# A graph and expert network on one core: expert results added to the output rows by accumulating transfers

## What is computed

```python
h = xf @ shared_w1 + shared_b1
z = swiglu5(h, ...) @ shared_w2 + shared_b2
w, idx = jax.lax.top_k(softmax(xf @ gate_w + gate_b), 2)     # w normalised to sum 1
cw = sum(one_hot(idx, 16) * w)
te = swiglu5(xf @ expert_w1[e] + expert_b1[e], ...)          # for every e
oe = te @ expert_w2[e] + expert_b2[e]
out = x + z + sum_e cw[:, e] * oe[e]
```

## Time and profile before

| what | value |
|---|---|
| median of 3 runs | 988.98 us (986.0 to 990.35) |
| the profiled execution, own time | 987.39 us |
| its span, first to last instruction | 985.6 us |
| PE busy (matmuls) | 853.1 us, 87% |
| DVE busy | 509.0 us, 52% |
| ACT busy | 234.1 us, 24% |
| POOL busy | 78.6 us, 8% |
| mean granted TensorE clock | 0.943 |
| HBM read, written | 101.97 MB, 16.92 MB |

### The profile page before, as it was taken

One profiled execution on the slowest core, in us unless ns is written; L12 is line 12 of the kernel. 1 busy time (PEld: TensorE's weight loads), 2 busy tenths in 40 slices (PEclk: granted clock), 3 DMA queues, 4 the chain that ended last, 5 costly groups with the idle time before them and its releaser, 6 DMA issues.

```text
span 985.6 us, 12333 instructions
## 1 busy us (share of the span) xinstructions
PE 853.1 (87%) x3638; PEld 572.8 (58%) x3639; DVE 509.0 (52%) x934; ACT 234.1 (24%) x483; POOL 78.6 (8%) x127
## 2 busy tenths in 40 slices
PE   4887699999999949679998688999998989999890
PEld 2444478888888826368887543544554545555440
DVE  7988681431431797890246958434343343433362
ACT  2555321431431024242112121102121211212110
POOL 2000000000000300000000010111011110110180
PEclk9999779999999978889999598999999999999996
DMA  4720000000000010001001120427754593314163
GB/s 141 223 101 1 1 1 1 0 1 1 1 1 1 27 45 1 1 1 43 1 3 60 66 91 0 168 99 276 279 176 154 190 352 92 148 53 154 39 178 118
DMA packets 38647, 80.98 MB, mean 82 GB/s; under 512 B 7304, under 2 KB 7554, under 8 KB 38602
## 3 DMA queue, kind: packets, MB, share of 16 engines
q1 hardware_dynamic: 27850, 60.55, 17.9%
q0 software_dynamic: 6720, 12.49, 4.3%
q10 hardware_dynamic: 4032, 7.34, 2.0%
HBM read 101.97 MB, written 16.92 MB: 121 GB/s over the span
## 4 chain that ended last, share of the span: by engine, by line
PE 70%; DVE 11%; DMA 5%; ACT 5%; issue 4%; POOL 2%; ACTq 1%; SPq 0%; DVEq 0%; POOLq 0%
PE PS L893 18%; PE PS L1108 13%; PE PS L923 8%; PE PS L1141 7%; PE PS L827 5%; PE PS L1016 5%; DMA WB<-in_b 3%; PE PS L962 3%; PE PS L1096 3%; PE PS L1126 2%; ACT CTR L607 1%; ACT YF L754 1%; POOL GA L576 1%; POOL GB L576 1%; DMA GB<-y_dram,slot_i 1%
## 5 line engine op out<-in xcount | busy, mean ns | idle before, releaser
L893 PE MATMUL PS<-CTR,YH 125*128 125x500 f32 (+1 forms) x480 | 167.0, 363 | 3.8 <-DVE YL L1405 3.4
L893 PE MATMUL PS<-CTR,YL 125*128 125x500 f32 (+1 forms) x480 | 165.1, 359 | 0.0
L1108 PE MATMUL PS<-WB,YF 128*128 x448 | 150.4, 489 | 7.5 <-DMA WB<-in_b 5.0
L1108 PEld LDWEIGHTS PS<-WB,YF 128*128 128x128 f32 x448 | 84.0, 190 | 76.7 <-issue 24.7
L893 PEld LDWEIGHTS PS<-CTR,YH 125*128 125x128 f32 x480 | 92.1, 192 | 22.5 <-DVE YL L1405 9.8
L893 PEld LDWEIGHTS PS<-CTR,YL 125*128 125x128 f32 x480 | 92.6, 193 | 12.6
L1141 PE MATMUL PS<-WB,YF 128*128 x168 | 79.4, 609 | 12.5 <-ACT YF L754 11.2
L827 PE MATMUL PS<-ET 125*128 125x130 f16 x494 | 71.0, 291 | 15.7 <-ACT CTR L607 8.2
L1438 DVE TENSOR_TENSOR ZL<-PS,ZH 128x500 fp32r<-128x500 f32 (+1 forms) x36 | 21.1, 591 | 93.1 <-ACT ZH L657 93.1
L754 ACT COPY YF<-PS 128x384 f32<-128x384 f32 (+1 forms) x38 | 18.1, 477 | 213.8 <-PE PS L1118 213.8
L827 PEld LDWEIGHTS PS<-ET 125*128 125x128 f16 x494 | 40.4, 116 | 47.0 <-ACT CTR L607 26.5
(11 more groups left out here) (324 smaller groups left out, 1214.8 us busy)
## 6 DMA issues: line engine op xcount, KB each, us to landing
WB<-in_w SPq DMA_DIRECT2D x28, 1536.0 KB
WB<-in_w SPq DMA_DIRECT2D x28, 768.0 KB
WB<-in_b SPq DMA_DIRECT2D x28, 384.0 KB
y_dram<-YF ACTq DMA_DIRECT2D x28, 256.0 KB
y_dram<-XTF SPq DMA_DIRECT2D x1, 4352.0 KB, 14.5
X<-in_x SPq DMA_DIRECT2D x1, 2500.0 KB
xn_dram<-XN SPq DMA_DIRECT2D x1, 2500.0 KB
out<-X SPq DMA_DIRECT2D x10, 250.0 KB
```

What stands on the lines that cost most here:

```text
L893: mm = nc.tensor.matmul(dest, lhs, rhs, start=(t == 0 and h == 0), stop=(t == NT - 1 and h == 1))
L1108: mm = nc.tensor.matmul(PS[:, 2 * k + h, 0:INTER], xgt[:, k, f, :], WB[:, bass.ds(off + (f * H2 + h * INTER), INTER)], start=(f == 0), sto ...
```

## The change

All ten shared blocks now come before the experts (`EARLY = NT`, 10). SP stores the ten tiles of `X` to `out` between the loads of the third and the fourth block's weights. The expert results no longer go to `y_dram`: POOL issues for each block one indirect transfer that adds the 128 rows of `yo` to their rows in `out` in memory. `out` gets 128 extra rows, one for each partition; an unused slot adds its zeros there. The extra rows are set to zero at the start and cut off on the host. Each such transfer waits for the one before (`scattered`), and each is issued behind the gather for the third next block (`AHEAD = 3`). ACT's `result` now waits for the transfer of two blocks before in place of the store. `GA`, `GB`, their gathers and sums, and `store` are gone. DVE works out the destination table `home` before it signals `tables_ready`.

```diff
-EARLY = 6
+EARLY = NT
+AHEAD = 3
...
-            sp.dma_start(y_dram[SURE * BS:NB * BS, :].rearrange("(b p) d -> p b d", p=BS),
-                         XT[:, 0:D].rearrange("p (o d) -> p o d", o=1).to_broadcast([128, NB - SURE, D])
-                         ).then_inc(zeroed, 16)
+            sp.dma_start(out[N:N + BS, :], XT[:, 0:D]).then_inc(zeroed, 16)
...
-            for b in range(4):
+            for b in range(NWB):
+                load_weights(b // 2, b % 2, b)
+            for t in range(NT):
+                sp.wait_ge(z_added, t + 1)
+                sp.dma_start(out[t * NP:(t + 1) * NP, :], X[0:NP, t, :]).then_inc(out_stored, 16)
+            for b in range(NWB, 4):
                 load_weights(b // 2, b % 2, b)
...
-            for t in range(NT):
-                sp.wait_ge(sum_ready, t + 1)
-                sp.dma_start(out[t * NP:(t + 1) * NP, :], X[0:NP, t, :]).then_inc(out_stored, 16)
+            sp.wait_ge(zeroed, 16)
             sp.wait_ge(out_stored, 16 * NT)
...
-            for b in range(2):
-                gather(0, b, b)
+            def scatter(k, b):
+                if isinstance(b, int):
+                    turn, seen = b + 1, 16 * b
+                else:
+                    turn, seen = pool.to_reg(b + 1), pool.to_reg(b * 16)
+                if not (isinstance(b, int) and b < 1):
+                    pool.wait_ge(scattered, seen)
+                pool.tensor_copy(dest_i[:, k:k + 1], home[:, bass.ds(b, 1)]).then_inc(dest_ready, 1)
+                pool.wait_ge(out_stored, 16 * NT)
+                pool.wait_ge(yo_ready, turn)
+                pool.wait_ge(dest_ready, turn)
+                pool.indirect_dma_start(out[:, :], bass.IndirectOffsetOnAxis(dest_i[:, k:k + 1], 0), yo[:, k, :], None,
+                                        compute_op=ALU.add).then_inc(scattered, 16)
+
+            for b in range(AHEAD):
+                gather(0, b % 2, b)
+            pool.wait_ge(zeroed, 16)
             last = last_pair(pool)
-            with pool.Fori(1, NB // 2) as i:
+            gather(0, 1, AHEAD)
+            scatter(0, 0)
+            with pool.Fori(2, NB // 2) as i:
                 with pool.If(i < last + 1):
-                    for k in range(2):
-                        gather(i, k, i * 2 + k)
-
-            all_stored = pool.to_reg(last * 16 + 16)
-            pool.wait_ge(tables_ready, 1)
-            pool.wait_ge(stored[0], all_stored)
-            pool.wait_ge(stored[1], all_stored)
-            for t in range(NT):
-                for k, dest in enumerate((GA, GB)):
-                    pool.indirect_dma_start(dest[0:NP, t, :], None, y_dram[:, :],
-                                            bass.IndirectOffsetOnAxis(slot_i[0:NP, k, t:t + 1], 0)
-                                            ).then_inc(back_in[t // 2], 16)
...
+                    gather(i, 0, i * 2)
+                    scatter(1, i * 2 - AHEAD)
+                    gather(i, 1, i * 2 + 1)
+                    scatter(0, i * 2 + 1 - AHEAD)
+            ending = pool.value_load(eb_i[0:1, 3, 1:2], min_val=SURE - AHEAD, max_val=NB - AHEAD)
+            for j in range(AHEAD):
+                scatter((j + 1) % 2, ending + j)
+            pool.wait_ge(scattered, pool.to_reg(last * 32 + 32))
...
                 act.wait_ge(y_done, b + (EARLY + 1))
                 if not first:
-                    act.wait_ge(stored[k], i * 16)
+                    act.wait_ge(scattered, act.to_reg(b * 16 - 16))
...
-            shared_up(0, last * 2 + (EARLY + 2), EARLY)
             turn_act(1, last * 2 + (EARLY + 1))
             down(last, 1, last * 2 + 1)
-            for j in range(NT - EARLY):
...
-            v.tensor_copy(wslot[:, :], PS[:, 4, NB:2 * NB]).then_inc(tables_ready, 1)
+            link(v.tensor_copy(wslot[:, :], PS[:, 4, NB:2 * NB]))
+            link(v.tensor_scalar(padrow, nodef[:, 0:1], float(N), None, ALU.add))
+            link(v.tensor_scalar(filled, wslot[:, :], 0.0, None, ALU.not_equal))
+            link(v.scalar_tensor_tensor(out=filled, in0=PS[:, 4, 0:NB], scalar=padrow, in1=filled,
+                                        op0=ALU.subtract, op1=ALU.mult))
+            v.tensor_scalar(home, filled, padrow, None, ALU.add).then_inc(tables_ready, 1)
...
-            def gathered_sum(t):
...
-            def last_sum(t):
...
-    out = nc.dram_tensor("out", (N, D), F32, kind="ExternalOutput").ap()
+    out = nc.dram_tensor("out", (N + BS, D), F32, kind="ExternalOutput").ap()
...
-    return r.results[0]["out"]
+    return r.results[0]["out"][0:N]
```

More of the change, by code:

```diff
@@ L160, in build @@
         assert R_ZL + NWB * WBUF * 4 <= R_SW and 2 * ROWB <= NWB * WBUF * 4
-        GA, GB = [at(n, r, [128, NT, D]) for n, r in (("GA", R_ZL), ("GB", R_ZL + ROWB))]
         used = [0]
@@ L265, in build @@
         tt_ps, tt_ready, y_done, yo_ready = sem("tt_ps"), sem("tt_ready"), sem("y_done"), sem("yo_ready")
-        stored = [sem("stored0"), sem("stored1")]
+        dest_ready, scattered = sem("dest_ready"), sem("scattered")
         zeroed = sem("zeroed")
@@ L269, in build @@
         cw_ps, cwt_ready = sem("cw_ps"), sem("cwt_ready")
-        back_in = [sem(f"back_in{g}") for g in range(NT // 2)]
-        sum_ready, out_stored = sem("sum_ready"), sem("out_stored")
+        out_stored = sem("out_stored")
         xn_dram = nc.dram_tensor("xn_dram", [N, D], F32, kind="Internal")
-        y_dram = nc.dram_tensor("y_dram", [NB * BS, D], F32, kind="Internal")
         w1f = FFNR[0:FK3, 0:W1C]
@@ L349, in build @@
         idx = sb("idx", [128, 2], I32)
+        dest_i = sb("dest_i", [128, 2], I32)
+        padrow, filled = rcarve(1), rcarve(NB)
+        home = rcarve(NB).bitcast(I32)
         idx_ready = sem("idx_ready")
@@ L572, in _ @@
-            pool.wait_ge(stored[0], all_stored)
-            pool.wait_ge(stored[1], all_stored)
-            for t in range(NT):
-                for k, dest in enumerate((GA, GB)):
-                    pool.indirect_dma_start(dest[0:NP, t, :], None, y_dram[:, :],
-                                            bass.IndirectOffsetOnAxis(slot_i[0:NP, k, t:t + 1], 0)
-                                            ).then_inc(back_in[t // 2], 16)
-            for g in range(NT // 2):
-                pool.wait_ge(back_in[g], 16 * 4)
+                    gather(i, 0, i * 2)
@@ L767, in sigmoid @@
                 nc.scalar.activation(ss[k][0:rows], hb[k][0:rows, 0:H2:2], ACT.Sigmoid, scale=alpha).then_inc(gate_sig, 1)
-            def store(i, k, b):
-                act.wait_ge(yo_ready, b + 1)
-                act.dma_start(y_dram[bass.ds(b * BS, BS), :], yo[:, k, :]).then_inc(stored[k], 16)
             def result(i, k, b, first=False):
@@ L793, in _ @@
                 with act.If(i < last + 1):
-                    store(i, 0, i * 2 - 2)
                     turn_t(1, i * 2 + (EARLY - 1))
@@ L801, in _ @@
                         result(i - 1, 1, i * 2 - 1)
-                    store(i, 1, i * 2 - 1)
                     turn_t(0, i * 2 + EARLY)
@@ L805, in _ @@
                     result(i, 0, i * 2)
-            store(0, 0, last * 2)
             turn_t(1, last * 2 + (EARLY + 1))
-            sigmoid(0, last * 2 + (EARLY + 2))
             result(last, 1, last * 2 + 1)
-            store(0, 1, last * 2 + 1)
-            for j in range(NT - EARLY):
-                turn_t(j % 2, last * 2 + (EARLY + 2 + j), NP)
-                if j + 1 < NT - EARLY:
-                    sigmoid((j + 1) % 2, last * 2 + (EARLY + j + 3))
         @block.tensor
@@ L1168, in _ @@
                 shared_up(p % 2, p, p)
-                if p == EARLY - 3:
+                if p == 3:
                     pe.wait_ge(slots_ready, 1)
@@ L1790, in _ @@
             link(v.tensor_scalar(ebf[0:1, 3, 0:1], ebf[0:1, 3, 0:1], -MAGIC, None, ALU.add))
-            link(v.tensor_copy(eb_i[0:1, 3, 0:1], ebf[0:1, 3, 0:1]))
+            v.tensor_copy(eb_i[0:1, 3, 0:1], ebf[0:1, 3, 0:1])
+            link(v.tensor_scalar(eb_i[0:1, 3, 1:2], ebf[0:1, 3, 0:1], 2.0, float(2 - AHEAD), ALU.mult, ALU.add))
             z_add(0, 0)
@@ L1797, in _ @@
             v.tensor_copy(tok[:, :], PS[:, 4, 0:NB])
-            v.tensor_copy(wslot[:, :], PS[:, 4, NB:2 * NB]).then_inc(tables_ready, 1)
+            link(v.tensor_copy(wslot[:, :], PS[:, 4, NB:2 * NB]))
[4 more added lines that the diff above has]
+            v.tensor_scalar(home, filled, padrow, None, ALU.add).then_inc(tables_ready, 1)
             dve.wait_ge(tables_ready, 1)
             last = last_pair(dve)
[L1801 to L1806, removed]
+            for p in range(4, EARLY):
+                z_add(p - 2, p - 2)
+                units(p % 2, p)
             rows_copy(0, 0)
@@ L1821, in _ @@
                     units(1, i * 2 + (EARLY + 1), i * 2 + 1, next_rows)
-            def gathered_sum(t):
-                dve.wait_ge(back_in[t // 2], 16 * 4)
-                link(v.tensor_tensor(GA[0:NP, t, :], GA[0:NP, t, :], GB[0:NP, t, :], ALU.add))
-            def last_sum(t):
```

## The result

The changed kernel takes **978.73 us**, the median of 6 runs (973.36 to 983.83), against 989.71 for six runs of the kernel before. The ratio is 0.9903, with a 95% interval of 0.9881 to 0.9925: faster by 0.75 to 1.2%. The forecast was 977. The profiled execution took 980.72 us; its span is 979.0, where 973.7 was forecast, at a mean granted clock of 0.943, as before. In medians the gain is 11.0 us, in the spans of the two profiled executions 6.6: that of the change lies 2.0 us above its median of 978.73, that of the kernel before 2.3 under its median of 989.71.

A forecast was written before the change was run, and what follows sets the result against it. TensorE was 70% of the chain, then a 58.6 us tail of gathers, sums and stores. Block 26's end, 916.82 + 40.8 + 2.8 = 960.4, plus two scatters gave span 973.7, 11.9 less; on the median's level 977, range 969 to 999.

The forecast's parts named there:

- Shared blocks, +40.8: Four shared blocks moved ahead of the experts delay the expert stage by 4 x 10.19 = 40.8 us, the change's price.
- What leaves the tail: 20 gathers, 11.27 us of landing, 20 additions and 10 stores leave the end; stores of X are covered before the next load.
- the 4.2: Last expert block: turn, copy and matmuls take 4.2 us after its activation chain, as for block 26.
- DVE's row table: Five small operations on DVE, about 1 us with waits, beside DVE's 1.99 us wait for TensorE: nothing paid.
- The fill: The fill of y_dram at the start shrinks to 128 rows; its waiter, ACT, comes long after: no effect.
- ACT's stores: ACT loses 28 stores, issued after results for which nobody on the chain waits: no effect.
- L = 5: Each adding scatter on POOL takes 5 us from issue to landing, range 3.2 to 11.3; the chain waits for data.
- the list of what would show it: Signs for the later profile: scatter landings of 4 to 8 us; wrong if POOL idles on its own scatter mid-stage.
- Traffic, 2.8 us: The adding pass lengthens four TensorE waits on weight loads by 0.7 us each, 2.8 us; range 0 to 8.4.
- The sum's last term: At the end, from the last scatter's landing at 973.3 to the span's end: 0.4 us for last wait and wakes.
- the slow one: Rival: POOL's chain of 28 scatters bounds the expert stage from a mean step of 9.54 us; slower, chance 0.22.
- Its variant on two engines: Scatters run on two DMA engines, L = 12, about 1080 us; chance 0.04 of the slow rival's 0.22.

The follow-up runs named there:

- x3: Kernel before with only the order changed: all ten shared blocks ahead of the experts, results still through y_dram, gathers and sums at the end; 1021.82 us, ratio 1.0343.
- x4: Changed kernel with the large fill of y_dram put back at its old place, nothing reading it; 980.54 us, ratio 0.9922 to the kernel before.
- x2: Changed kernel with the scatters as plain writes, without the addition; 973.93 us, ratio 0.9865 to the kernel before.
- x1: Changed kernel with the last wait for the scatters on ACT, with one tiny copy behind it, not on POOL; 973.08 us, ratio 0.9859 to the kernel before.
- x5: Changed kernel with four weight buffers, the fourth in the place of the dead shared weights; 967.10 us, ratio 0.9783 to the kernel before.
- x7: Changed kernel with AHEAD = 2, each scatter issued one gather earlier; 1125.68 us, ratio 1.1393 to the kernel before.
- x6: Changed kernel with four weight buffers, the last wait on ACT, and seven idle transposes on TensorE between the last two blocks' matmuls; 965.93 us, ratio 0.9767.
- x8: Changed kernel with four weight buffers and the last wait on ACT, without extra transposes; 966.50 us, ratio 0.9773 to the kernel before.

## Why the prediction was right

The verdict and the size hold: 977 against 978.73, and no rival came. That the two are so near is luck in part: between the profiled executions the span fell by 6.6 us where 11.9 was forecast. By steps:

1. **Shared blocks, +40.8.** Right. The cadence is 10.19 to 10.20 us to the last of them. The stage starts 38.3 us later; step 4 accounts for the other 2.5. That these blocks "cost the tail almost nothing" where they stood was not quite so (x3), but enters no term.
2. **What leaves the tail.** Right in kind. The stores of `X` were all issued by 698.6, and the next load of new weights came at 707.5, as soon as block 0's second matmuls were done (707.1). Block 27's matmuls end at 967.44, not at 921.2 + 43.6 = 964.8, for three small reasons: 0.75 us to wake TensorE for the turn, which the 4.2 left out; ACT's copy starts 0.75 us after the turn (at block 26 it is at once), behind passes of its loop for blocks that this input doesn't have; and the last six matmuls took 4.34 us. So ACT's result decided the last issue and not the scatter before, and it came 0.8 later than the sum has it.
3. **DVE's row table.** Nothing, as said: no wait for it in the list.
4. **The fill.** "Nothing" was wrong by some 3 us in the profiles, in the kernel's favour (x4). The step that failed is the view on which it rests: I looked for who waits for the fill, not for what runs beside it.
5. **ACT's stores.** Nothing, as said.
6. **L = 5.** Right where no load runs (4.6 to 5.0). The 4.7 worked out beside the rule on adding transfers in "Collectives: The Full Stack" of the Trainium skill, section "The bandwidth ceiling: the fold count and why AG ≠ RS ≠ AR", is as near. That section is about reductions between cores and says nothing of POOL's issue; here the issue takes 1.60 us with the addition and 1.00 without (x2). Beside loads L is up to 9.5, and "4 to 8" in the list of what would show it was too low. Two of the signs named there as wrong did appear: POOL bound by its own scatter (eight times) and ACT waiting for one (six times). No wait of TensorE comes from them, since late landings stand among short ones: the mean from issue to the next copy is 6.8, plus 1.0 to the next issue, 7.8 against 9.54 (estimates, from the mean of 27 steps).
7. **Traffic, 2.8 us.** Near, by luck in part. Over the stage's 248.0 the profile of the change has 5.1 us, x4's 3.8 and x1's 1.0, mean 3.3. The term was mis-sized twice, with opposite signs: the addition costs 1.1 us of all 16 engines each time and not 0.7 (6.3 us of the stage by x2's one profile), and without it the stage is 3.0 shorter than before.

The sum's last term, 0.4 from the last landing to the end, failed: it measured 979.0 - 973.9 = 5.1, of which 4.65 are POOL's drain. The drain's row was in the trace of before too, but there SP's last stores ended 9 us later and hid it.

The profiled span is 5.3 above the forecast's 973.7: 4.7 for that term and 0.8 for the last issue, less 0.2 for an L of 4.8; the stage's 2.3 more and the start's 2.5 less cancel. Of the rivals the slow one is closed by L: twelve landings are of 8.2 us or more, but the mean step stays 1.7 us under the 9.54 from which it decides. Its variant on two engines has L = 12, where a scatter that runs alone lands in 4.6 to 5.0. It also falls with the windows around the scatter of block 26 (columns as in the earlier trace rows):

```profile
964.00:965.00 1.00, 1.00 (x3) 0.37 (x2) 0.00 (x0) 0.00 (x0) 0.00 (x0) 0.50 1.15 125
965.00:966.00 1.00, 1.00 (x3) 0.48 (x2) 0.00 (x0) 0.00 (x0) 0.00 (x0) 0.50 0.78 133
```

No load runs here. The engines move 125 and 133 GB/s, as much as the 127 that five reached, and the share is 1.15 and 0.78 of all 16 (above 1 since a packet that waits counts too, by my reading). By the rule of the Trainium skill, "DMA: Bandwidth & Descriptors", section "Why a DMA increments its semaphore by 16 and not by 1", it would be 2 of 16. As for the gather in the earlier trace rows, the trace disagrees.

## What to carry to other kernels

A result that several producers add up can be added in memory as each is ready, instead of gathered again at the end; it pays where the adding transfers hang behind each other with slack, and where the work pulled ahead to allow it costs less than the tail it removes. On an engine that issues both, everything that a later stage waits for goes ahead of a transfer that waits for a result: turned round, it cost 147 us. When work leaves the tail, read every queue's last instructions in the old trace, and look at what memory the new order frees: here the fourth buffer was worth as much as the change.

## What the runs showed of the hardware

- POOL's closing drain took 3.99 us (before) and 4.65 (the change, x2, x4, x5, x7) once its transfers had landed, and 7.3 to 7.4 us (x1, x6, x8) when begun 0.2 to 0.3 us ahead of the last one's issue, in which case the span ended 2.5 us earlier.
- An indirect scatter of 128 rows of 2 KB that adds in memory lands in 4.6 to 5.0 us alone and in 8.2 to 9.5 beside a load of weights. It costs 1.60 us on POOL (1.00 without the addition) and, against the same scatter without it, 1.1 us of all 16 engines in packet time.
- The fill of 17 blocks of 256 KB on SP goes with two idle gaps of ACT of 1.66 to 1.85 us for which the profile shows no wait, in three profiles of three; the seven profiles without it have none. The cause is open.
- TensorE's granted clock fell to 0.50 (the 1.2 GHz level) at the last matmuls of the change, after 0.92 and 1.44 us of idleness around the turn; x5 had the same two and stayed at the upper level, 2.4 GHz. x1 and x8 both had 0.89 and 1.47, and their last six matmuls took 4.53 and 2.84 us. Idle time of that size alone doesn't decide it.
